# Four DRAM-to-DRAM weight copies issued after the first part of the kernel instead of inside it

## What is computed

```
x = x + tanh(g_xattn) * xattn(layernorm(x), ctx, ctx)
x = x + tanh(g_ffn)   * ffn(layernorm(x))

def xattn(x, k, v):                      # 4 heads of 128
    Q, K, V = x @ Wh, k @ Wh, v @ Wh     # per head
    masked = (Q K^T / sqrt(128)) * decay_mask
    A = max(abs(masked.sum(over the 64 sequences)), 1)
    Y = layernorm(A @ V) * gamma + beta
    return (relu(x @ wg_w) * Y) @ wo_w

def ffn(x):                              # 1408 inner units
    h = silu(x @ gate_w.T * gate_s) * (x @ up_w.T * up_s)
    return (h @ down_w.T) * down_s
```

## Time and profile before

| | |
|---|---|
| median of 3 runs | 1491.2 us (1488.97 to 1491.81) |
| profiled execution, its own time | 1487.68 us |
| its span | 1485.8 us |
| PE busy | 1471.6 us, 99% of the span |
| DVE, POOL, ACT busy | 1028.7, 724.4, 709.9 us |
| bytes moved by DMA | 321.79 MB, mean 217 GB/s |

### The profile page before, as it was taken

The page is one execution under the profiler, slowest core; times in us unless marked ns, Lnnn a source line. Parts: engine busy times, 40 slices in busy tenths (PEclk is TensorE's granted clock), DMA queues, the critical chain, the costliest instruction groups (busy, mean ns, idle before and its releaser), DMA issues.

```text
span 1485.8 us, 20243 instructions
## 1 busy us (share of the span) xinstructions
PE 1471.6 (99%) x7132; PEld 1046.8 (70%) x7132; DVE 1028.7 (69%) x1514; ACT 709.9 (48%) x1127; POOL 724.4 (49%) x709
## 2 busy tenths in 40 slices
PE   8999999999999999999999999999999999999998
PEld 6888888878667767677777767766566666666665
DVE  7777877778567666666667676654768768668662
ACT  5555555554655545355453544433344344343442
POOL 6656767742444535354353544434138137237236
PEclk9999999999999999999999999999999999999999
DMA  8999999983988687877878787775483472572422
GB/s 297 374 327 357 319 351 338 329 289 97 290 218 246 174 234 224 229 219 182 260 213 225 228 210 227 190 200 144 119 219 111 138 218 96 143 205 95 140 101 86
DMA packets 367286, 321.79 MB, mean 217 GB/s; under 512 B 259088, under 2 KB 285200, under 8 KB 366992
## 3 DMA queue, kind: packets, MB, share of 16 engines
q1 hardware_dynamic: 349616, 288.49, 63.3%
q10 hardware_dynamic: 17568, 31.99, 6.1%
HBM read 216.09 MB, written 117.31 MB: 224 GB/s over the span
## 4 chain that ended last, share of the span: by engine, by line
PE 92%; DVE 3%; DMA 2%; ACT 1%; issue 1%; POOL 1%; SPq 0%; ACTq 0%; DVEq 0%
PE ps L1915 16%; PE ps L1913 15%; PE pyb L1787 10%; PE po L1787 5%; PE ps L1833 5%; PE ps L1922 4%; PE ps L1920 4%; PE po L1915 4%; PE po L1913 4%; PE pyb L1903 4%; PE ptb L1903 4%; PE pyb L1922 3%; PE ptb L1922 3%; PE ptb L1920 3%; PE pyb L1920 3%; PE pyb L1907 2%
## 5 line engine op out<-in xcount | busy, mean ns | idle before, releaser
L1693 POOL TENSOR_TENSOR hid_low<-tmp,reg 128x512 f16<-128x512 f32 x88 | 117.9, 1341 | 132.2 <-ACT reg L797 132.2
L1787 PE MATMUL pyb<-reg,xreg 128*128 128x512 f32 x708 | 177.9, 396 | 0.0
L1673 POOL TENSOR_TENSOR p5b<-p5b,p1b 128x512 f32<-128x512 f32 x44 | 56.4, 1283 | 215.5 <-ACT p5b L821 215.5
L1684 POOL TENSOR_TENSOR hsp<-hall,hsp 128x640 f16<-128x640 f32 (+2 forms) x72 | 136.3, 1908 | 33.2 <-ACT hsp L848 32.1
L1787 PEld LDWEIGHTS pyb<-reg,xreg 128*128 128x128 f32 x708 | 129.0, 189 | 24.7
L868 ACT ACTIVATE tmp<-ps,colsb 128x512 f32<-128x512 f32 x88 | 60.5, 688 | 162.4 <-PE ps L1915 81.3
L1337 DVE SCALAR_TENSOR_TENSOR tmp<-ps,colsb,tmp 128x512 f32<-128x512 f32 x88 | 65.6, 746 | 78.2 <-PE ps L1913 42.9
L1650 POOL TENSOR_TENSOR wyt<-raw,wyt 128x1024 fp32r<-128x1024 f32 x30 | 74.0, 2467 | 85.3 <-ACT wyt L786 85.3
L1915 PE MATMUL ps<-op,wbuf 128*128 128x512 f32 x352 | 103.9, 417 | 0.0
L1915 PE MATMUL ps<-reg,gate 128*128 128x512 f32 x352 | 103.4, 416 | 0.0
L1833 PEld LDWEIGHTS ps<-reg 128*128 128x128 f32 x768 | 98.0, 191 | 6.2 <-ACT tmp L698 1.5
(11 more groups left out here) (195 smaller groups left out, 3319.3 us busy)
## 6 DMA issues: line engine op xcount, KB each, us to landing
wbuf<-ws_scratch SPq DMA_DIRECT2D x44, 896.0 KB, 4.9
xr<-in_x SPq DMA_DIRECT2D x62, 512.0 KB, 6.2
raw<-in_ctx_t SPq DMA_DIRECT2D x32, 512.0 KB, 6.7
v_scratch<-tmp ACTq DMA_DIRECT2D x64, 256.0 KB, 6.4
raw<-v_scratch SPq DMA_DIRECT2D x32, 512.0 KB, 6.4
x_scratch<-xr SPq DMA_DIRECT2D x32, 512.0 KB, 4.5
xr<-x_scratch SPq DMA_DIRECT2D x32, 512.0 KB, 5.7
raw<-w_scratch SPq DMA_DIRECT2D x31, 512.0 KB, 6.3
```

The costliest lines, as they stand in the source:

```text
L1684: e.tensor_tensor(hsp[t % 2][1][:, i0:i1, :], hall[:, i0:i1, 128 * i:128 * i + 128], f(hsp[t % 2][0][:, i0:i1, :]), ALU.subtract).then_inc ...
L1693: e.tensor_tensor(hid[1][:, m % 11, :], tmp[:, m % 3, :], f(hid[0][:, m % 11, :]), ALU.subtract).then_inc(s["hlo"])
L1787: last = e.matmul(dst, lhs[a], rhs[b], start=(k == 0 and i == 0), stop=(k == n - 1 and i == 2))
```

## The change

Chunks 8 to 11, the copies of w_down, are no longer issued in the loop at g = 8 to 11. Chunks 8 and 9 are issued behind the loop, ahead of the store of tile LATE; chunks 10 and 11 behind the store of tile LATE + 5. Nothing else is altered: the same twelve copies, the same waits inside `weights_chunk` (chunks 8 and 9 wait for four earlier copies of their parity, 10 and 11 for five), and the same `down_load`.

```diff
             for g in range(1, NG):
                 more = g + 1 < NG
-                if g < 12:
+                if g < 8:
                     weights_chunk(g)
...
+            weights_chunk(8)
+            weights_chunk(9)
             w_store(LATE)
             x_again(1)
             v_load(2)
...
             w_store(LATE + 4)
             w_store(LATE + 5)
+            weights_chunk(10)
+            weights_chunk(11)
             v_load(4)
```

## The result

In 14 timed executions of each kernel, taken together, the changed kernel's median is 1492.55 us (1490.41 to 1498.31) and that of the kernel before 1489.58 us (1488.46 to 1492.41). The ratio is 1.0019 with a 95% interval of 1.0011 to 1.0026: 2.8 us slower, 1.6 to 3.9. The forecast was no change. In one later set three of the 33 timed executions of the kernel before took 2494 to 5318 us; they are left out of every comparison. The profiled execution of the changed kernel took 1489.8 us of span, 4.0 more than that of before.

A forecast was written before the change was run, and what follows sets the result against it. PE's own time was taken to bound the kernel, with saturated DMA engines beside it. Terms of 0 + 0 + 0 (at most 0.7 + 2.5) left 1487.7 us profiled, 1491.2 for the median; range 1488.8 to 1493.9.

The forecast's parts named there:

- the stated range: Range for the changed kernel's median, 1488.8 to 1493.9 us, including slow copies at the top and run spread below.
- The forecast's own range: Range for the median under the main forecast, a move under 0.7 us: 1489.5 to 1492 us; chance 0.66.
- Who else uses the DMA engines then? First the two v stores.: Chunks 8 and 9 ahead of tile LATE's store: other transfers stay covered; cost taken as 0, at most 0.7 us.
- Behind it.: Transfers from y_out on, behind chunks 10 and 11: shifted 0.8, 2.2 or 5.2 us; w_load's 4.4 us covers two cases.
- The loop: Four copies leaving g = 8 to 11: PE waits for none of the loads there, so gain 0.
- A copy was taken at 2.6 us: Moving 0.72 MB at the new places: between 1.9 and 4.1 us, taken as 2.6; 5.2 for a pair.
- PE's limit at 375.5: Latest landing of v_load(4) that costs PE nothing, counted back from the hidden that PE needs at about 378.7.
- The gate: down_load(0) at 378.82 waits for all copies; forecast no wait. Rival: late copies hold SP there, 1494.6 us, chance 0.09.
- The Trainium skill's rate: 207 to 214 GB/s per direction for HBM copies: an estimated 3.4 us a copy, v_load(4) landing at an estimated 376.5.
- The slow rate: Rival: slow copies land v_load(4) at 376.5 to 378.0, PE waits 1.0 to 2.5 us; 1492.2 to 1493.7; chance 0.18.
- The faster one: Rival: lightening saturated groups returns at most the 3.5 us by which unprofiled executions are slower: 1487.7 us; chance 0.07.
- The slower side: Outcome slower beyond 0.2%, chance 0.09: copies hold SP at down_load(0), deciding from a landing of 16.6 us.

The follow-up runs named there:

- one pair ahead: Against the kernel before, only chunks 10 and 11 leave the loop, issued ahead of the store of tile LATE; 1489.81 us, 0.4 over (-0.9 to 1.9).
- the pair just behind LATE: Against the kernel before, only chunks 10 and 11 leave the loop, issued behind tile LATE's store and x_again(1), at about 334.1; 1489.12 us.
- four copies: Against the kernel before, chunks 8 to 11 are all issued behind the store of tile LATE + 5; 1496.63 us, 6.0 over (3.7 to 8.3).
- all four copies in the holes: Against the kernel before, chunks 8 and 9 go behind the store of tile LATE + 2, 10 and 11 behind that of LATE + 3; 1489.88 us.

## Why the prediction was wrong

The measured median lies in the stated range, but the kernel is slower, by a difference that its measurement tells from none, where no move was forecast. That it lies in the range is in part luck: the range stands around 1491.2 us, the median of three executions, and the median of before in the 14 is 1489.58. The forecast's own range, 1489.5 to 1492, doesn't hold it. The sentence that nothing under 3 us can be told from no change was wrong too; 14 executions of each told 2.8.

Two steps failed, and both are omissions.

**"Who else uses the DMA engines then? First the two v stores."** The list was not complete. I weighed the stores at 323.74 and 324.33 and tile LATE's store on SP's queue, but not the store of tile LATE - 1, which ACT issues at 328.87, 1.5 us behind the copies, and whose landing the `w_out` at 336.45 asks for. It had 3.6 us to spare (332.9 to 336.45), and the copies cost it 4.9. What is left after the slack is absorbed down ACT's and DVE's queues to 0.36 to 0.77 us at PE, in the five traces with two whole copies there. The traces show this stall; the timed runs of one pair ahead (0.4 us, -0.9 to 1.9) can't tell it from nothing. Shown: it vanishes with the pair 7 us later, with the pair behind it on ACT's queue, with one copy in place of two. What has not been measured is which mechanism holds the store. My reason for safety, that one queue's transfers are worked off one behind another, holds for SP's queue and says nothing of ACT's.

**"Behind it."** The shift of 2.2 us that I gave the transfers was right: `y_out` landed 2.4 us late (379.2, less the 2.44 us by which PE was behind at C, against 374.3). What was wrong is where I looked for its slack. I took the first `w_load`, with 4.4 us, and stopped. The row for the second was in the trace: DVE had been idle 6.49 us, waiting for that load, when it multiplied at 401.86. From there ACT ended its rounding at 405.95 for PE at 408.38, and POOL its subtraction at 410.3 for PE at 412.0: 2.4 and 1.7 us to spare. The load came 3.1 us late (407.3 less 2.44, against 401.8), and 1.6 us of that reached PE.

The lateness didn't stay constant on the way, as I had let it. It was 2.4 us at the first `y_out`, but only 0.5 when the next `y_in` was issued (393.46 less 2.44, against 390.49): SP waits there for DVE's multiplication by the first `w_load`, which stood at 389.19 before and came 0.5 us late, and this wait swallowed the rest. Then the lateness came back. The issue of that `y_in`'s four transfers took 5.17 us in place of 3.17, and the load behind them landed after 7.4 us in place of 6.7. In all three traces of the changed kernel and the three with one pair behind LATE + 5 or behind `v_load(4)` this issue took 4.7 to 5.2 us, with the DMA engines at share 1.04 to 1.09 in its first 3 us. In seven of the eight others in the table above it took 2.9 to 3.7 us at share 0.65 to 0.88; the pair just behind LATE had 4.92 us at share 1.03. So it looks as if what the copies added to the backlog was still there at this issue, 20 us behind C, and showed as SP's time to issue; the traces show the two together, not which makes which. The experiments add that the loads of w_down were nearly as tight.

**What held.** The loop gave nothing back. A copy was taken at 2.6 us; the two copies behind LATE + 5 landed at 374.3 and 376.6, 2.3 apart. `v_load(4)` was forecast at 375.0 with PE's limit at 375.5; it landed at 377.8, 375.3 without the shift, and PE's wait for L1341 is 0.74 as before. With four copies the limit was passed and PE waited 4.08 us there. The gate didn't hold SP: the copies had landed at 376.6, `down_load(0)` was issued at 383.21. The Trainium skill's rate (DMA: Bandwidth & Descriptors, Latency and other measured facts), by which PE would have waited an estimated 1.0 us at this place, is not borne out: 2.3 us a copy is 0.31 MB per us.

**The rivals.** None is what happened. The slow rate and the gate name other places. The faster one rested on 3.5 us between the profiled execution and a median of three; with 14 it is 1.9, and the lighter loop gave nothing back. The slower side was right in sign, and its chance of 0.09 was too low because I tied it to one mechanism that needed a landing of 16.6 us.

**What stays open.** The traced stalls sum to 2.28, 1.63 and 2.30 us, mean 2.1; the timed difference is 2.8 (1.6 to 3.9). The two agree within the interval. What could add to them is a later start-up, which the three traces of the changed kernel have; against it speaks the run with all four copies in the holes, which leaves the loop in the same way and has the median of before (0.1 us, -1.2 to 1.6). Why a store on ACT's queue waits for SP's copies, even for pieces issued after it, isn't settled. Neither is why SP's issue takes longer beside full DMA engines, nor why the clock falls after some of PE's waits and not after others of the same length.

## What to carry to other kernels

An empty stretch of the DMA engines is not enough: list every transfer issued or still in flight from the place on, on all queues, with the instruction that waits for it and its slack, and go on until the engines have been idle once. In this kernel the same four copies cost nothing 12 and 16 us away. The row to look for is a busy engine's own idle time before a consumer "<-DMA" (here 6.49 us of DVE): it says that the transfer is already what sets this instruction, and only the slack behind it is left. Plotting the landing against the stretch over many traces, as in the table above, finds both the transfer and its slack. And don't carry one lateness down a queue: here it shrank to 0.5 us at a wait and grew to 3.1 behind it.

## What the runs showed of the hardware

- A 256 KB store on ACT's queue landed after 3.4 to 4.0 us, 6.6 with one 704 KB DRAM-to-DRAM copy on SP's queue beside it, 8.6 to 9.0 with two, and 8.5 with the two cut into eight transfers of which five were issued later than the store. The 4.6 to 5.6 us that it paid for two whole copies are no less than the 4.6 that two copies took elsewhere (2.3 us apart). Issued 1.6 us ahead of the copies on the same queue it paid nothing (4.0).
- Four loads of 128 KB took SP 2.9 to 3.7 us to issue with the DMA engines at share 0.65 to 0.88 beside them, and 4.7 to 5.2 us at share 1.03 to 1.09, in the 14 traces of the table. Outside it stand 3.3, 3.4 and 4.5 us at shares 0.78, 0.96 and 0.88.
- The granted clock fell to 0.50 after some waits of PE and not after others: in eight of 17 traces after a wait of 1.8 to 2.3 us near 38, but not after 2.5 us there or after 2.37 us at 110.36. From the last us of a wait of 4.08 us it was 0.50 for some 6 us, and C to D lost 2.7 us on top of the wait.
- The same instructions up to 143 us, with the DMA engines at share 0.98 in the kernel before (33 to 143), put PE's group there anywhere from 142.6 to 148.1 in 17 traces, and the first `o` from 333.7 to 339.5. A single profile's span can't carry a claim of 2 us here; stretches between fixed points, which repeat to 0.01 to 0.02 us where nothing is late, can.
